# Cross attention with keys on partitions, scores made twice, in one loop with the experts

## The chip, the core and the metric

The kernel is one program on one core of a Trainium2 chip. It computes a two-layer decoder block by block. The metric is the device time of one execution in microseconds. The change touches the last two blocks of the program; all that comes before them is the same code.

## What is computed

Only the end of the reference matters here: layer 1's cross attention and its experts, each followed by a residual and a layer norm (post-norm). There are 8 sequences (B = 8) of 256 tokens (S) with 512 channels (D). x is the decoder's state, ctx the context, both 256 x 512 for a sequence.

The cross attention runs over channels, not over tokens: `_L1_xattn_ref` reads q, k and v as (sequence, 256 rows, 512 columns), splits the 256 rows into 8 heads of 32, and attends from the 512 columns of q to the 512 columns of k:

```
qh = q.reshape(B, h, 32, 512); kh, vh alike (k = v = ctx)
qk = einsum('bhdq,bhdl->bhql', qh, kh) / sqrt(32)
ret = einsum('bhql,bhdl->bhdq', softmax(qk), vh)      # 8 heads, 512 x 512 scores each
x = layernorm(x + gamma * ret)
```

The experts (`_L1_ffn_ref`) project each token with 8 router columns and 8 x 16 hidden columns (136 in all), take a softmax over the 8, keep the best 2, scale the hidden values by the gates, multiply by a 128 x 512 matrix, add biases, and the result goes through residual and layer norm once more.

## The kernel before

Every engine has its own hand-written instruction list, which runs in order; semaphores tie the lists together. The blocks follow one another with a barrier of all engines between two of them.

**Cross attention, `l1_cross` (L1794).** A tile is 128 rows of x, that is 4 heads (HT = 4); a sequence has T = 2 tiles. Exact products are made by splitting fp32 numbers into a rounded part (hi) and the rest (lo); `stack` (L1877) copies them by 32 DMAs per sequence on SyncE's queue into qs and ks, four blocks of 32 rows on top of each other, so that one fp32r matmul with 128 rows gives the exact score. A sequence has STEPS = 16 steps. A step takes 256 queries of one head: `scores` (L2090) makes two 128 x 512 blocks with the queries on partitions; VectorE's `maxima` (L2013) reduces 1024 columns to two negated maxima; ScalarE's `exps` (L1965) makes exp(s - max) with accumulated row sums; two steps later TensorE turns the 8 blocks p by transposes (`turn`, L2100), ScalarE and VectorE copy half each to SBUF (L1973, L2020), and `values` (L2124) multiplies them in fp32, four heads packed on 32-column tiles, in parts spread over the steps. At the end of a tile the reciprocals of 16 sums per partition (L2025) are spread over columns by small matmuls (L2109), `scale_out` multiplies (L2031) and adds the residual (L2036), statistics (L221, L225) and `apply` (L239) normalise, GpSimd takes the power (L231, L233), and SyncE stores x to DRAM. Score PSUM has two buffers of two banks; v_ps and m_ps have one bank each.

**Experts, `l1_experts`.** Its loads begin behind the barrier. Per sequence: `turn_x` (L2373, 8 transposes), copies (L2255), `project` (L2382, 8 fp32 matmuls of 136 columns), `shift` (L2284 to L2289), `exponential` (L2260), `route` (L2295 to L2330), `turn_hidden` (L2390), copies (L2266, L2267), `out` (L2399, L2400: 4 fp32 matmuls of 512 columns), residual (L2341), norm, store.

A fp32 matmul stands in the trace as two records, a transpose or an fp32r matmul as one.

## Time and profile before

| | us |
|---|---|
| median of 3 runs | 2082.64 (2082.24 to 2092.4) |
| the profiled execution | 2083.66 |
| its span, first to last instruction | 2081.9 |
| TensorE, VectorE, ScalarE, GpSimd busy in the span | 1846.4, 1249.2, 920.4, 288.0 |
| cross block, from 1629.75; experts block, first instruction at 1993.88 | to 1990.75; to 2081.9 |

Engines are named PE (TensorE matmuls), PEld (its weight loads), DVE (VectorE), ACT (ScalarE), POOL (GpSimd) and SPq (SyncE's DMA queue). Matmul ends are modelled, so a matmul's real spacing is read from the starts. "Idle before" names what ended the wait. The granted clock is a share of 2.4 GHz; 0.5 is the lower of its two levels, 1.2 GHz.

### The profile page before, as it was taken

Reading aid. Unit: us, or ns where it says so; the run is one execution under the profiler, and the core shown is the slowest. Engines: PE = TensorE matmul, PEld = TensorE weight load, DVE = VectorE, ACT = ScalarE, POOL = GpSimd, SP = SyncE. Lnnn points to the kernel's source line nnn. Section 1 sums busy time; section 2 is a strip of 40 time slices with the busy share of each in tenths; the row PEclk is TensorE's granted clock in tenths of the full one; section 3 lists DMA queues with packets and bytes.
Section 4 is the critical chain, followed back from the end, with each engine's and each line's share of the span. In section 5 each row is a group of like instructions: output and inputs, shape, how many; then the busy total and the mean of one; then the engine's idle time right before and its main releaser. Section 6 shows DMA issues by size and latency. Waiting matters only on the chain. (4 is left out here: it accounts for less than half of the span.)

```text
span 2081.9 us, 33021 instructions
## 1 busy us (share of the span) xinstructions
PE 1846.4 (89%) x12272; PEld 1503.4 (72%) x12272; DVE 1249.2 (60%) x2330; ACT 920.4 (44%) x2376; POOL 288.0 (14%) x347
## 2 busy tenths in 40 slices
PE   6979999999976799999999996799997498889966
PEld 5868999998964588888888985677775365555543
DVE  3446444444434565546555536788887288878847
ACT  2224333333323343333333223666666288878811
POOL 0000000000002111111111001333343111121001
PEclk9989999999997799999999998999998699999988
DMA  3122000000013231111101013000010675556234
GB/s 104 45 97 72 21 21 21 21 21 21 10 48 101 66 97 47 36 31 41 46 19 34 11 41 121 11 31 32 31 42 21 182 179 136 153 140 149 68 114 142
DMA packets 86253, 136.62 MB, mean 66 GB/s; under 512 B 9480, under 2 KB 25480, under 8 KB 86096
## 3 DMA queue, kind: packets, MB, share of 16 engines
q1 hardware_dynamic: 86096, 134.52, 22.3%
q8 instruction: 99, 1.62, 0.3%
q14 instruction: 58, 0.48, 0.1%
HBM read 79.88 MB, written 21.05 MB: 48 GB/s over the span
## 5 line engine op out<-in xcount | busy, mean ns | idle before, releaser
L1164 PE MATMUL yp<-ccy,toep 128*128 128x288 f32 x640 | 182.4, 436 | 19.5 <-POOL ccy L892 13.4
L1965 ACT ACTIVATE e_p<-e_s_ps,e_nb 128x512 f32<-128x512 f32 x256 | 175.0, 696 | 51.6 <-DVE e_nb L2013 49.5
L2013 DVE TENSOR_REDUCE e_nb<-e_s_ps 128x2 f32<-128x1024 f32 x128 | 155.8, 1218 | 54.3 <-PE e_s_ps L2090 53.5
L1442 ACT ACTIVATE p<-p,nb,rq 128x128 f32<-128x128 f32 (+1 forms) x256 | 137.0, 541 | 94.5 <-DVE nb L1539 94.5
L2100 PE MATMUL e_t_ps<-ident,e_p 128*128 128x128 f32 x1024 | 148.7, 284 | 24.7 <-DVE e_pT L2020 13.2
L1164 PEld LDWEIGHTS yp<-ccy,toep 128*128 128x128 f32 x640 | 126.5, 206 | 55.7 <-POOL ccy L892 14.8
L2100 PEld LDWEIGHTS e_t_ps<-ident,e_p 128*128 128x128 f32 x1024 | 120.8, 146 | 62.5 <-issue 52.9
L80 PE MATMUL q_ps<-a_xt_hi,wq_hi 128*128 128x256 f32 x512 | 151.7, 296 | 4.1 <-DVE wo_lo L112 4.1
L1062 DVE SCALAR_TENSOR_TENSOR hm<-gu_ps,us_col,sg 128x256 f32<-128x256 f32 x88 | 42.3, 481 | 182.3 <-ACT sg L971 182.3
L82 PE MATMUL q_ps<-a_xt_hi,wq_lo 128*128 128x256 f32 x512 | 146.5, 286 | 0.0
L81 PE MATMUL q_ps<-a_xt_lo,wq_hi 128*128 128x256 f32 x512 | 146.4, 286 | 0.0
L514 ACT ACTIVATE ex<-ex 128x512 f32<-128x512 f32 x64 | 40.5, 632 | 213.8 <-DVE ex L567 213.8
L231 POOL TENSOR_TENSOR n_rstd<-n_mv,eps 128x2 f32<-128x2 f32 x32 | 6.3, 197 | 895.9 <-DVE n_mv L225 895.9
L971 ACT ACTIVATE sg<-gu_ps,gs_col 128x256 f32<-128x256 f32 x88 | 41.6, 473 | 188.3 <-PE gu_ps L82 188.3
L545 DVE TENSOR_TENSOR tl<-t_ps,th 128x512 fp32r<-128x512 f32 x64 | 44.3, 692 | 132.6 <-ACT th L506 132.6
L1399 POOL TENSOR_TENSOR p<-p,rs 128x512 f32<-128x512 f32 x64 | 94.2, 1472 | 194.5 <-DVE rs L1546 194.5
L2090 PE MATMUL e_s_ps<-ks,qs 128*128 128x512 f32 x256 | 97.5, 464 | 12.6 <-DMA ks<-e_cl 11.5
L80 PE MATMUL o_ps<-wo_hi,th 128*128 128x512 f32 x256 | 106.7, 417 | 1.9 <-DVE tl L545 1.9
L80 PE MATMUL gu_ps<-m_xt_hi,wg_hi 128*128 128x256 f32 x352 | 100.2, 285 | 8.2 <-DVE m_xt_lo L1054 8.2
L567 DVE TENSOR_SCALAR ex<-q_ps,bq_col 128x256 f32<-128x256 f32 x128 | 55.8, 477 | 80.0 <-PE q_ps L82 80.0
L80 PEld LDWEIGHTS q_ps<-a_xt_hi,wq_hi 128*128 128x128 f32 x512 | 99.8, 195 | 4.5 <-issue 4.5
L81 PE MATMUL o_ps<-wo_lo,th 128*128 128x512 f32 x256 | 101.2, 395 | 0.0
(277 smaller groups left out, 5122.1 us busy)
## 6 DMA issues: line engine op xcount, KB each, us to landing
x_after<-n_r SPq DMA_DIRECT2D x24, 512.0 KB, 3.0
toep<-padded_kernels SPq DMA_DIRECT2D x32, 256.0 KB, 3.5
qs<-e_xh SPq DMA_DIRECT2D x64, 128.0 KB, 2.5
qs<-e_xl SPq DMA_DIRECT2D x64, 128.0 KB, 2.6
ks<-e_ch SPq DMA_DIRECT2D x64, 128.0 KB, 2.6
ks<-e_cl SPq DMA_DIRECT2D x64, 128.0 KB, 2.6
x<-x_after SPq DMA_DIRECT2D x12, 512.0 KB, 4.7
x<-in_x SPq DMA_DIRECT2D x8, 512.0 KB, 4.1
```

What stands on the lines that cost most here:

```text
L80: pe.matmul(out, whi, xhi, start=start, stop=False)
L81: pe.matmul(out, whi, xlo, start=False, stop=False)
L82: return pe.matmul(out, wlo, xhi, start=False, stop=stop)
L545: dve.tensor_tensor(tl[:], t_ps[:], th[:], ALU.subtract).then_inc(tl_done, 1)
L567: dve.tensor_scalar(ex[p % 2][:, h, :], q_ps[p % 2][:, h, :], bq_col[:, head:head + 1], 0.0, ALU.add, ALU.min).then_inc(mq_done, 1)
L1164: last = pe.matmul(yp[:, lo % 2, 0:NCOL], toep[h % 2][:, (lo - li) * P:(lo - li + 1) * P], ccy[h % 2][:, li, 0:NCOL], start=(li == 0), sto ...
L1399: pool.tensor_tensor(tile, tile, r, ALU.mult).then_inc(pn_done, 1)
L1442: act.activation(p[n % 3][:, h, part[t]], p[n % 3][:, h, part[t]], ACT.Exp, bias=nb[i][:, t, h:h + 1], scale=rq[u][:, t:t + 1], accum_out= ...
L1965: act.activation(pr[i][:, a, :], s_ps[i][:, a, :], ACT.Exp, bias=nb[i][:, a:a + 1], accum_out=sums[t][:, j, q:q + 1]).then_inc(e_done, 1)
L2013: dve.tensor_reduce(nb[i][:], s_ps[i][:], AX.X, ALU.max, negate=True).then_inc(nb_done, 1)
L2090: last = pe.matmul(s_ps[i][:, a, :], qs[u][:, h // HT, h % HT, q * P:(q + 1) * P], ks[u][:, h // HT, h % HT, :], start=True, stop=True)
L2100: last = pe.transpose(t_ps[a][:, k, :], pr[m % 2][:, a, k * P:(k + 1) * P], core.ident[:])
```

## The change

`l1_cross` and `l1_experts` become one function with one loop, `l1_cross_and_experts`. Scores are made twice. The rough pair: two fp32r matmuls of the rounded parts alone (32 rows, on 32-row tiles) with queries on partitions, only for `maxima`. The negated maxima are turned by 4 transposes per tile (`turn_largest`), rounded by ScalarE, and written by 4 row DMAs on ScalarE's queue (`place_largest`) into row 97 of qs, against a row of ones in ks. The exact scores (97 rows, three blocks: hi hi, lo hi, hi lo, and the maximum) are then made with keys on partitions, so that `exps` makes p already turned and needs neither bias nor accumulation. `values` multiplies it (4 fp32 matmuls) and `ones` (4 more) gives the sums, in d_ps; both banks are single. VectorE's `normalise` takes a reciprocal of 128 x 512 and one product.

A sequence has again 16 steps. At step g TensorE issues the rough pair of step g+11, the two score matmuls of step g, and at odd steps `values` for four earlier score blocks. The rough pairs share two PSUM buffers (a_ps) with all the rest: context, maxima, x, hidden, turned and out. They alternate in the order of `slot_uses`; `take` waits until the last use of the buffer has been read. Of the diff, the core (VectorE's and ScalarE's unchanged helpers are left out):

```diff
-STEPS = HX * NQ // 2
-HALF = STEPS // 2
+STEPS = T * NQ * HT // 2
+UNITS = 2 * STEPS
+LEAD = 11
+NPT = 12
+KX = 3 * CX + 1
...
+        a_ps = [pb(f"e_a_ps{i}", [P, 2, D]) for i in range(2)]
+        s_ps = [pb(f"e_s_ps{i}", [P, D]) for i in range(2)]
+        v_ps, d_ps = pb("e_v_ps", [P, D]), pb("e_d_ps", [P, D])
...
+        def steps():
+            for b in range(-1, B + 2):
+                for step in range(STEPS):
+                    g = STEPS * b + step
+                    if -LEAD <= g <= STEPS * (B + 1) + 5:
+                        yield b, step, g
...
+                def stack(b):
...
+                    for j in range(HT):
+                        for dst, plan in ((qs, (xh[b % 2], xl, xh[b % 2])), (ks, (ch[b % 2], ch[b % 2], cl))):
+                            for r, src in enumerate(plan):
...
             @block.gpsimd
             def _(pool):
...
+                for b, step, g in steps():
+                    if step == 3 and 0 <= b - 2 < B:
+                        power(b - 2, mv6, mv6_done, y6_done, rstd6, ve6_done, rstd6_done)
+                    if step == 3 and 0 <= b - 1 < B:
+                        residual(b - 1, 1)
+                    if step == 6 and 0 <= b - 1 < B:
+                        power(b - 1, mv5, mv5_done, y5_done, rstd5, ve5_done, rstd5_done)
+                    if step == 6 and b + 2 < B:
+                        scale_x(b + 2)
+                    if step == 10 and b + 2 < B:
+                        take_lo(pool, b + 2, "cl")
+                    if step == 11 and 0 <= b < B:
+                        residual(b, 0)
+                    if step == 12 and b + 2 < B:
+                        take_lo(pool, b + 2, "xl")
...
             @block.scalar
             def _(act):
...
+                def place_largest(n):
...
+                    for j in range(HT):
+                        act.dma_start(qs[b % 2][KX - 1:KX, t, j, :].bitcast(F32),
+                                      nbr[n % 2][j * CX:j * CX + 1, :].bitcast(F32)).then_inc(biased, 16)
...
+                for b, step, g in steps():
+                    if step == 1 and 0 <= b - 2 < B:
+                        hidden(b - 2)
+                    if step in (6, 14) and 0 <= 2 * b + 1 + step // 8 < 2 * B:
+                        place_largest(2 * b + 1 + step // 8)
+                    if 0 <= g < PAIRS_IN_ALL:
+                        exps(2 * g)
+                        exps(2 * g + 1)
+                    if step == 4 and 0 < b + 1 < B:
+                        context(b + 1)
+                    if step in (5, 13) and 0 <= 2 * b + 1 + step // 8 < 2 * B:
+                        round_largest(2 * b + 1 + step // 8)
+                    if step == 9 and 0 <= b - 1 < B:
+                        turned(b - 1)
+                    if step == 9 and b + 2 < B:
+                        round_hi(b + 2, "ch")
+                    if step == 11 and b + 2 < B:
+                        round_hi(b + 2, "xh")
+                    if step == 12 and 0 <= b - 1 < B:
+                        exponential(b - 1)
...
             @block.vector
             def _(dve):
...
+                def normalise(n):
+                    dve.wait_ge(pv_mm, NQ * (n + 1))
...
+                    dve.reciprocal(rec[:], d_ps[:]).then_inc(rec_done, 1)
...
+                    dve.scalar_tensor_tensor(rb[n % 2][:], v_ps[:], gcol[:, 0:1], rec[:], ALU.mult, ALU.mult)\
+                       .then_inc(o_scaled, 1)
...
+                for u in range(2):
+                    dve.memset(ks[u][KX - 1:KX, :, :, :].bitcast(F32), 1.0).then_inc(set_up, 1)
+                take_lo(dve, 0, "cl")
+                take_lo(dve, 0, "xl")
...
+                for b, step, g in steps():
+                    if step == 2 and 0 <= b - 2 < B:
+                        add_experts(b - 2)
+                    if step == 11 and 0 <= b - 1 < B:
+                        shift(b - 1)
+                    if 0 <= g + LEAD < PAIRS_IN_ALL:
+                        maxima(g + LEAD)
+                    if b == 0 and step == 0:
+                        dve.wait_ge(w_loaded, 64)
...
+                    if step in (2, 10) and 0 <= 2 * b - 1 + step // 8 < 2 * B:
+                        normalise(2 * b - 1 + step // 8)
+                    if step == 2 and 0 <= b - 2 < B:
+                        statistics(b - 2, added6, b - 1, st6, st6_done, mv6, mv6_done)
+                    if step == 4 and 0 <= b - 2 < B:
+                        apply(b - 2, mv6, rstd6, rstd6_done, y6_done)
+                    if step == 5 and 0 <= b - 1 < B:
+                        statistics(b - 1, added5, T * b, st5, st5_done, mv5, mv5_done)
+                    if step == 7 and 0 <= b - 1 < B:
+                        apply(b - 1, mv5, rstd5, rstd5_done, y5_done)
+                    if step == 13 and 0 <= b - 1 < B:
+                        gate(b - 1)
+                        choose(b - 1)
+                    if step == 14 and 0 <= b - 1 < B:
+                        picks(b - 1)
+                        weigh(b - 1)
...
             @block.tensor
             def _(pe):
...
+                def take(kind, n, *freed):
+                    i = place[kind, n] % 2
+                    if read[i]:
+                        pe.wait_ge(*read[i])
+                    read[i] = freed
+                    return a_ps[i]
...
+                def rough_scores(n):
...
+                    bank = take("pair", n, nb_done, n + 1)
+                    for i in range(2):
+                        j = 2 * jj + i
+                        d = slice(j * CX, (j + 1) * CX)
+                        last = pe.matmul(bank[:, i, :], xh[b % 2][d, t, q * P:(q + 1) * P], ch[b % 2][d, t, :],
+                                         start=True, stop=True, skip_group_check=True, tile_position=(j * CX, 0))
...
+                def scores(u):
...
+                    if u >= 2:
+                        pe.wait_ge(e_done, u - 1)
+                    pe.matmul(s_ps[u % 2][:], ks[b % 2][0:KX, t, j, k * P:(k + 1) * P], qs[b % 2][0:KX, t, j, :],
+                              start=True, stop=True).then_inc(s_mm, 1)
...
+                def values(n):
+                    b, t, k, _ = unit(HT * n)
+                    pe.wait_ge(e_done, HT * (n + 1))
+                    if k == 0 and n:
+                        pe.wait_ge(o_scaled, T * b + t)
...
+                for b, step, g in steps():
+                    if 0 <= g + LEAD < PAIRS_IN_ALL:
+                        rough_scores(g + LEAD)
+                    if 0 <= g < PAIRS_IN_ALL:
+                        scores(2 * g)
+                        scores(2 * g + 1)
+                    if g == 1:
+                        pe.wait_ge(set_up, 5)
+                    if g % 2 and 0 <= (g - 3) // 2 < T * NQ * B:
+                        values((g - 3) // 2)
+                    if step == 1 and 0 <= b - 2 < B:
+                        out(b - 2)
+                    if step == 3 and 0 < b + 1 < B:
+                        turn_context(b + 1)
+                    if step in (5, 13) and 0 <= 2 * b + 1 + step // 8 < 2 * B:
+                        turn_largest(2 * b + 1 + step // 8)
+                    if step == 8 and 0 <= b - 1 < B:
+                        turn_x(b - 1)
+                    if step == 10 and 0 <= b - 1 < B:
+                        project(b - 1)
+                    if step == 15 and 0 <= b - 1 < B:
+                        turn_hidden(b - 1)
```

The store of x behind the cross attention and its reload are gone: the residual stays in SBUF (rr). The router's weights and biases are loaded behind the first sequence's stack.

## Rows read from the trace of the kernel before

**Rows 1.** Windows: length, busy PE, PEld, DVE, ACT, POOL, clock, DMA share, GB/s
```profile
1629.00:1986.00 357.00, 301.60 (x2368) 191.56 (x2368) 273.23 (x346) 277.19 (x688) 57.48 (x38) 0.93 0.55 139
1986.00:2082.00 96.00, 62.30 (x288) 41.26 (x288) 58.51 (x241) 15.46 (x40) 8.85 (x21) 0.84 0.41 138
```

**Rows 2.** Groups by line, cross block: count, busy us, mean ns, idle before
```profile
L1965 ACT ACTIVATE e_p<-e_s_ps,e_nb 128x512 f32<-128x512 f32 x256 | 175.0, 696 | 51.6 <-DVE e_nb L2013 49.5 <-PE e_t_ps L2100 1.8
L2013 DVE TENSOR_REDUCE e_nb<-e_s_ps 128x2 f32<-128x1024 f32 x128 | 155.8, 1218 | 54.3 <-PE e_s_ps L2090 53.5 <-ACT e_p L1965 0.6
...
L2020 DVE COPY e_pT<-e_t_ps 128x512 f32<-128x512 f32 x128 | 87.2, 681 | 10.6 <-PE e_t_ps L2100 10.6
L1973 ACT ACTIVATE e_pT<-e_t_ps 128x512 f32<-128x512 f32 x128 | 77.5, 605 | 13.1 <-PE e_t_ps L2100 12.4
...
L1965 ACT ACTIVATION_READ_ACCUMULATOR e_p<-e_s_ps,e_nb 128x1 f32 x256 | 54.3, 212 | 0.0
```

**Rows 3.** Timeline, two steps of cross attention: start us, duration us, instruction
```profile
1955.15 0.30 PEld L2090 LDWEIGHTS e_s_ps<-ks,qs 128*128 128x128 f32 x2 [0.84 <-ACT e_p L1965]
...
1955.92 1.22 DVE L2013 TENSOR_REDUCE e_nb<-e_s_ps 128x2 f32<-128x1024 f32 x1 [0.74 <-PE e_s_ps L2090]
...
1958.45 0.16 PEld L2124 LDWEIGHTS e_v_ps<-e_pT,e_vt 128*32 128x32 f32 x8 [0.17 <-issue]
...
1958.52 0.59 ACT L1973 ACTIVATE e_pT<-e_t_ps 128x512 f32<-128x512 f32 x1
...
1959.00 0.70 ACT L1965 ACTIVATE e_p<-e_s_ps,e_nb 128x512 f32<-128x512 f32 x1
1959.44 0.30 PEld L2090 LDWEIGHTS e_s_ps<-ks,qs 128*128 128x128 f32 x2 [0.84 <-ACT e_p L1965]
```

**Rows 4.** TensorE behind two idle times (timeline), and a window behind the first
```profile
1781.95 1.93 PE L2124 MATMUL e_v_ps<-e_pT,e_vt 128*32 128x512 f32 x8 [3.17 <-DVE n_r L2036]
...
1782.00:1790.00 8.00, 8.00 (x37) 4.70 (x38) 5.30 (x6) 5.21 (x14) 0.00 (x0) 0.62 0.82 189
...
1930.48 0.63 PE L2100 MATMUL e_t_ps<-ident,e_p 128*128 128x128 f32 x4 [1.29 <-DVE e_pT L2020]
1931.04 1.07 PE L2124 MATMUL e_v_ps<-e_pT,e_vt 128*32 128x512 f32 x8
```

**Rows 5.** Timeline, experts: routing's first and last, copy, project, statistics
```profile
2012.23 0.17 DVE L2295 TENSOR_REDUCE f_den<-f_ex 128x2 f32<-128x16 f32 x1 [0.58 <-ACT f_ex L2260]
...
2015.09 0.49 DVE L2330 SCALAR_TENSOR_TENSOR f_hw<-f_lh,f_w 128x128 f32<-128x128 f32 x2
...
2024.50 1.08 ACT L2255 ACTIVATE f_xT<-f_x_ps 128x512 f32<-128x512 f32 x2 [4.34 <-PE f_x_ps L2373]
...
2025.64 2.12 PE L2382 MATMUL f_h_ps<-wrd,f_xT 128*128 128x136 f32 x16 [0.30 <-ACT f_xT L2255]
...
2025.87 1.27 DVE L221 BATCH_NORM_STATS2 n_stats<-n_r 128x6 f32<-128x512 f32 x2
```

**Rows 6.** Timeline, the last tile's values, back to back
```profile
1981.95 3.62 PE L2124 MATMUL e_v_ps<-e_pT,e_vt 128*32 128x512 f32 x32
```

**Rows 7.** Timeline, scores of four heads on 32-row tiles in the block before
```profile
1501.69 0.94 PE L1701 MATMUL s_ps<-kT,qT 32*128 32x128 f32 x16
```

**Rows 8.** An issue on SyncE's queue (timeline), and a DMA: KB, us to landing
```profile
1642.31 0.60 SPq L1886 DMA_DIRECT2D qs<-e_xh  x1
...
f_bias<-in_bd SPq DMA_DIRECT2D x1, 64.0 KB, 6.0
```

**Rows 9.** Groups by line: the reciprocals of 4 and of 16 columns
```profile
L1546 DVE RECIPROCAL rs<-sums 128x4 f32<-128x4 f32 x64 | 10.7, 168 | 0.2 <-ACT p L1442 0.2
L2025 DVE RECIPROCAL e_rs<-e_sums 128x16 f32<-128x16 f32 x16 | 3.9, 243 | 0.0
```

**Rows 10.** Timeline, the cross block's start: the last lo part, the first scores
```profile
1634.56 2.46 POOL L1866 TENSOR_TENSOR e_xl<-x,e_xh 128x1024 fp32r<-128x1024 f32 x1 [2.72 <-ACT e_xh L1948]
...
1644.22 0.93 PEld L2090 LDWEIGHTS e_s_ps<-ks,qs 128*128 128x128 f32 x3 [8.43 <-DMA ks<-e_cl]
```

More of the change, by code:

```diff
@@ new lines, in slot_uses @@
+        def slot_uses(b, step, g):
+            if 0 <= g + LEAD < PAIRS_IN_ALL:
+                yield "pair", g + LEAD
+            if step == 1 and 0 <= b - 2 < B:
+                yield "out", b - 2
+            if step == 3 and 0 < b + 1 < B:
+                yield "context", b + 1
+            if step in (5, 13) and 0 <= 2 * b + 1 + step // 8 < 2 * B:
+                yield "largest", 2 * b + 1 + step // 8
+            if step == 8 and 0 <= b - 1 < B:
+                yield "x", b - 1
+            if step == 10 and 0 <= b - 1 < B:
+                yield "hidden", b - 1
+            if step == 15 and 0 <= b - 1 < B:
+                yield "turned", b - 1
@@ new lines, in l1_cross_and_experts, with slot, unit, pair @@
+        place = {("context", 0): 0}
+        for at in steps():
+            for use in slot_uses(*at):
+                place[use] = len(place)
+        def slot(kind, n):
+            return a_ps[place[kind, n] % 2]
+        def unit(u):
+            b, rest = divmod(u, UNITS)
+            t, rest = divmod(rest, UNITS // 2)
+            return b, t, rest // HT, rest % HT
+        def pair(n):
+            b, rest = divmod(n, STEPS)
+            t, rest = divmod(rest, STEPS // 2)
+            return b, t, rest // 2, rest % 2
@@ L2269, in body @@
-                def body(b, u, first, last):
-                    if not last:
-                        turned(b + 1, 1 - u)
-                    if not first:
-                        hidden(b - 1, 1 - u)
-                    exponential(b)
-                turned(0, 0)
-                over_batches(act, body, lambda b, u: hidden(b - 1, 1 - u))
+                    if b:
+                        act.wait_ge(o_mm, b)
+                    bank = slot("turned", b)
+                    act.activation(hwT[:], bank[:, 0, 0:S], ACT.Copy).then_inc(hT_done, 1)
@@ L2344, in body @@
-                def body(b, u, first, second):
-                    shift(b, u)
-                    if not first and not second:
-                        norm.apply(dve, b - 2)
-                    route(b)
-                    if not first:
-                        residual(b - 1, 1 - u)
-                dve.wait_ge(w_loaded, 64)
-                dve.tensor_scalar(bias[:, 0, 0:E], bias[:, 0, 0:E], BONUS, None, ALU.add).then_inc(prepared, 1)
-                dve.wait_ge(prepared, 3)
-                def tail(b, u):
-                    norm.apply(dve, b - 2)
-                    residual(b - 1, 1 - u)
-                    norm.apply(dve, b - 1)
@@ L2360, in _, with add_experts @@
-                for b in range(B):
-                    body(b, b % 2, b == 0, b == 1)
-                tail(B, 0)
+                def add_experts(b):
+                    dve.wait_ge(o_mm, b + 1)
+                    dve.tensor_tensor(rr[b % 2][:], slot("out", b)[:], rr[b % 2][:], ALU.add).then_inc(added6, 1)
+                for u in range(2):
+                    dve.memset(ks[u][KX - 1:KX, :, :, :].bitcast(F32), 1.0).then_inc(set_up, 1)
+                take_lo(dve, 0, "cl")
+                take_lo(dve, 0, "xl")
@@ new lines, in turn_x, with project @@
+                def turn_x(b):
+                    pe.wait_ge(y5_done, T * b + T)
+                    bank = take("x", b, xT_done, b + 1)
+                    for k in range(KT):
+                        for t in range(T):
+                            last = pe.transpose(bank[:, k // 2, (k % 2 * T + t) * P:(k % 2 * T + t + 1) * P],
+                                                rr[b % 2][:, t, k * P:(k + 1) * P], core.ident[:])
+                    last.then_inc(x_turned, 1)
+                def project(b):
+                    pe.wait_ge(xT_done, b + 1)
+                    pe.wait_ge(w_loaded, 64)
+                    bank = take("hidden", b, lh_done, b + 1)
+                    n = E + E * R
```

656 lines of the change are left out of this document (250 added, 406 removed).

## The prediction

> **What bounds the kernel now.** I read the windows first: the cross attention block takes 357 us and the experts 96 us of a span of 2081.9 us [rows 1]; what comes before 1629 us is untouched. Then the groups by line in the cross block: ScalarE carries most, 175.0 us of exponentials, 54.3 of accumulator reads (partly beside them) and 77.5 of copies; VectorE has 155.8 us of maxima and 87.2 of copies [rows 2]. Then two steps of the loop in order of time [rows 3]: they take 4.29 us (weights of the scores at 1955.15 and 1959.44), and the circle is score pair, maximum of 1.22 us, exponentials, copy. TensorE does its transposes and values beside it. From the first scores at 1644.2 [rows 10] to the last values at 1985.6 [rows 6] eight sequences take 42.7 us each; the experts add 12 each with their start and end.
>
> **The change part by part.** It removes per step 8 transposes, both p copies and the accumulator reads; per sequence 8 of 32 stack DMAs and x's store and reload; and one block's start and end. It adds per step a rough pair (R), per two steps 8 fp32 matmuls for values and sums (V, 4 before), per sequence two reciprocals of 128x512, 8 transposes and 8 row DMAs for the maxima, and puts the experts into the same loop. So the time has to be made anew: I walk one sequence of 16 steps, each engine in its written order. P(s) is the start of TensorE's step s.
>
> *Prices, TensorE.* Four packed value matmuls cost 0.86 us (32 records of 16 matmuls in 3.62 us, less the last one's drain) [rows 6], 0.99 up to the next full tile's weights [rows 3]; so V is 1.71 and 0.14 for the change of tile. Two score matmuls are 0.47 and 0.1 of exposed weights. R is not in the trace. Its bounds are 0.47, two serial 512-column matmuls, and 0.235, two at once. The nearest row has four heads on 32-row tiles: 16 records, 3072 columns at two cycles, in 0.94 us where one after the other would take 2.56 at 2.4 GHz [rows 7]. They overlap, so I take 0.235, and 0.27 for two changes of tile. A step without V (E) is then 1.06 us of TensorE, one with V (O) 2.9. Eight transposes are 1.0, project 2.0 [rows 5], out 8 records of 0.43, 3.45.
>
> *ScalarE.* An exponential without accumulation lasts 0.6 and the next starts 0.48 later, as the copies [rows 3]; a product is read 0.29 us after its stream (pair weights 1955.15, read 1955.92). With two score banks the last two scores of an E,O pair wait for exponentials: +0.44, so a pair takes 4.4 us. A 1024-column copy is 1.08 [rows 5], the two hidden ones 0.7. The row DMAs of the maxima are issued ahead of exponentials; SyncE's issues take 0.60 for 32 rows [rows 8], below could be nought; I take 0.4 each for a single row, 1.6 for four.
>
> *VectorE.* A maximum (m) is 1.22, so 1.04 ns a column (1218 against 681 ns) [rows 2]; adding 1024 columns 1.25; statistics 1.66; apply 1.0; shift 0.9; gates to weights 3.4 [rows 5]. *Reciprocal:* 4 columns take 168 ns, 16 take 243 [rows 9], 6.25 ns a column more, so 512 take 0.243+496x0.00625=3.35 us. Its bounds are an ordinary pass of 0.68 and 243/16 ns a column, 7.8 us. I take 3.35, the only slope shown. With the product N=3.35+0.06+0.69=4.1.
>
> *The full sequence.* R leads TensorE's queue and shares two slots, so a late reader stops everything: the lead of 11 steps in data is none in slots.
> Steps 10, 11: m ends at 1.8, N at 5.9. TensorE does E, project, R and scores by 4.2; then V opens a new tile and waits for o_scaled, since v_ps and d_ps are single. P(12)=P(10)+7.85.
> 12 to 15: two pairs 8.8, maxima's transposes 0.55, hidden's 0.55, ScalarE's DMA issues 1.55: 11.45. VectorE, with routing in steps 13 and 14, keeps up.
> 0: R of step 1 needs the slot of "turned", which ScalarE copies behind two exponentials: 2.7.
> 1: O and out, 6.45.
> 2, 3: add to 1.45, m to 2.65, N to 6.75, statistics to 8.4, m to 9.6, for which R of step 4 waits; V waits for N (6.8+1.75+context 1.0): 9.65.
> 4: R of step 5 waits for the context copy behind two exponentials, 3.1. Step 5: 3.45. Steps 6, 7: 4.4+1.55. Steps 8, 9 with turn x and the wait for its copy: 5.2.
> The sum is 55.8 us. GpSimd's pieces, under 3 us each like the one in [rows 10], end before their readers' steps; if a residual were late, only statistics would move. SyncE's 24x0.64=15.4 us of stack issues are hidden in a sequence.
>
> *Ends.* The block starts at 1629.75. VectorE first fills two rows of 4096 columns, 4.2 us each at 1.04 ns (one partition; nought if faster), then makes both lo parts, ready at 1640.7 instead of 1637.0 [rows 10]. The stacks are issued by 1656.2; 8 maxima, transposes, copy, issues and landing end about there too: P(0)=1657. Sequence 0 takes 49.5, of it 6.5 for VectorE's wait at step 0 for the router's bias, issued last, with 6.0 to land [rows 8]. Sequence 1 takes 50.1 (no out, no hidden copies), 2 to 6 take 279, 7 takes 48.3 (no R behind step 4). Then the serial chain N, statistics, apply, turn, project, route, out, statistics, store: 43. Sum 2126.9, with 1.8 around the span 2128.7.
>
> *Clock.* Behind 3.17 us of idle the values take 1.93 us instead of 1.07 and the granted clock is 0.62 over the next 8 us; behind 1.29 us nothing falls [rows 4]. The walk has TensorE idle for 4.7 us in step 3 of sequences 1 to 7, and 1.8 in step 11. V and context at 1.2 GHz cost 2.7 more and the rest of the step 0.3: 7x3.0=21. For step 11, between the two rows, I put 0.7x8: together 27. Forecast: 2155 us, against 2083.66 of the profiled run (median 2082.64).
>
> **The rivals.** (1) *Cheap normaliser and free DMA issues.* With an ordinary-speed reciprocal N is 1.45: 16x2.65=42 off; with free issues 15x1.55=23 off; no clock drops: 2064, faster. For it: every reciprocal in the trace is tiny. Against: 243 ns for 16 columns is above such a floor, and an issue has always had a price on SyncE. It decides once N is under about 2.3 us, where V no longer waits in step 11. (2) *The cheap normaliser alone:* 2087, no change. (3) *No clock falls,* other waits breaking up the idle: 2129. Against: 3.17 us was enough. (4) *R doesn't overlap:* its matmuls run one after the other, 0.235 more in 128 steps, some hidden in ScalarE's waits, 26: 2181. [rows 7] speaks against. (5) *The rough pair truly runs ahead and nothing waits,* so that TensorE's own work sets the time, 8x41 us a sequence between 1657 and 43 of tail: 2030. The single v_ps speaks against, and the maxima behind N. (6) *The reciprocal's slope is hidden by a floor:* 4-column ones may stand at it, and eight ordinary passes, 8.3 ns a column, are 4.4 us: 16 more, 2171.
> The Trainium skill, VectorE: DVE Perf Modes, in "First, the fixed hardware budget", says that reciprocal is an iterative divide with a repeat count of 8. That would be rival 6; no row here shows a wide reciprocal.
>
> **How the numbers follow.** Forecast 0.50; rival 6 0.15; rival 3 0.13; rival 4 0.08; rival 2 0.05; rivals 1 and 5 together 0.09. Upwards the reciprocal's upper bound adds 16x4.5=72 (2227), DMA issues of 0.6 add 12. The range of 2080 to 2225 leaves out rivals 1 and 5 and what lies above. A measurement of this kernel tells 0.5%, 10 us, from no change. Faster, under 2072: 0.10; within: 0.06; slower: 0.84.
>
> **What would show it.** In the profile after: two reciprocals a sequence of 3.35 us each; V's weights idle until the normaliser is done, 4 to 5 us in step 3 and about 2 in step 11; R held by maxima and by ScalarE's copies; about 56 us from one sequence to the next; first scores at 1657; a granted clock below 1 behind step 3. It fails if a sequence takes under 50 us (cheap reciprocals, or the waits overlap better than a walk in single file has them), if R takes 0.5 us, or if ScalarE's exponentials don't feel the DMA issues.

## The result and the profile after

The changed kernel takes 2219.16 us (median, 2213.76 to 2229.92), the kernel before 2086.91 us beside it: a ratio of 1.064, 95% interval 1.059 to 1.069. It is slower by 132 us, on the side that the prediction gave 0.84, and inside its range, 6 us below the upper end. The forecast of 2155 is 64 us too low. The profiled execution is the slowest of them, 2229.92 us with a span of 2228.1.

The groups by line of the new block (count, busy us, mean ns, idle before and its releaser) show first what carries it. The reciprocals answer to [rows 9], the maxima and exponentials to [rows 2]:

```profile
L2147 DVE RECIPROCAL e_rec<-e_d_ps 128x512 f32<-128x512 f32 x16 | 53.6, 3349 | 11.2 <-PE e_d_ps L2332 11.2
...
L2141 DVE TENSOR_REDUCE e_nbx<-e_a_ps 128x2 f32<-128x1024 f32 x128 | 154.2, 1222 | 188.9 <-PE e_a_ps L2299 188.7
L2085 ACT ACTIVATE e_pT<-e_s_ps 128x512 f32<-128x512 f32 x256 | 139.1, 595 | 318.7 <-PE e_s_ps L2317 277.7
```

VectorE and ScalarE both wait for TensorE now. The windows of the first sequence's start and of four full sequences (length, then busy PE, PEld, DVE, ACT and POOL, clock, DMA share, GB/s) answer to [rows 1]:

```profile
1657.00:1701.00 44.00, 31.68 (x122) 11.18 (x122) 13.39 (x13) 14.69 (x26) 8.88 (x4) 0.67 0.67 175
1832.00:1903.00 71.00, 56.78 (x248) 21.90 (x248) 36.84 (x56) 23.13 (x42) 12.53 (x10) 0.78 0.30 75
1903.00:1971.00 68.00, 53.78 (x245) 20.62 (x244) 36.62 (x54) 22.79 (x42) 10.85 (x10) 0.80 0.31 78
1971.00:2039.00 68.00, 53.61 (x243) 20.32 (x242) 36.28 (x55) 22.54 (x41) 10.35 (x10) 0.80 0.26 63
2039.00:2107.00 68.00, 53.80 (x246) 20.66 (x245) 36.52 (x55) 21.87 (x41) 7.29 (x8) 0.80 0.26 63
```

A sequence takes 68.2 us where the walk had 55.8, at a mean granted clock of 0.80 against 0.93 before. The clock has two levels, so 0.80 means that TensorE stood at 1.2 GHz for 40% of the time, some 27 of 68 us. TensorE's part of the timeline (start us, duration us, instruction, the idle time before it with its releaser) shows where, from step 10 of one sequence to step 8 of the next:

```profile
1907.14 1.55 PE L2329 MATMUL e_v_ps<-e_pT,e_vt 128*32 128x512 f32 x8 [1.85 <-DVE e_rb L2151]
1908.39 2.01 PE L2332 MATMUL e_d_ps<-e_pT,e_ones 128*32 128x512 f32 x8
...
1913.16 1.07 PE L2329 MATMUL e_v_ps<-e_pT,e_vt 128*32 128x512 f32 x8
1914.05 1.04 PE L2332 MATMUL e_d_ps<-e_pT,e_ones 128*32 128x512 f32 x8
...
1919.52 0.98 PE L2317 MATMUL e_s_ps<-qs,ks 97*128 97x512 f32 x2 [2.33 <-ACT e_pT L2085]
...
1921.37 1.96 PE L2332 MATMUL e_d_ps<-e_pT,e_ones 128*32 128x512 f32 x8
...
1927.10 0.50 PE L2299 MATMUL e_a_ps<-e_ch,e_xh 32*128 32x512 f32 x2 [1.49 <-ACT f_wT L2106]
...
1928.23 1.94 PE L2329 MATMUL e_v_ps<-e_pT,e_vt 128*32 128x512 f32 x8
...
1941.92 1.93 PE L2329 MATMUL e_v_ps<-e_pT,e_vt 128*32 128x512 f32 x8 [4.02 <-issue]
...
1949.47 0.50 PE L2299 MATMUL e_a_ps<-e_ch,e_xh 32*128 32x512 f32 x2 [1.95 <-ACT e_vt L2061]
...
1950.57 1.06 PE L2329 MATMUL e_v_ps<-e_pT,e_vt 128*32 128x512 f32 x8
...
1956.94 0.98 PE L2317 MATMUL e_s_ps<-qs,ks 97*128 97x512 f32 x2 [2.33 <-ACT e_pT L2085]
...
1966.01 1.94 PE L2329 MATMUL e_v_ps<-e_pT,e_vt 128*32 128x512 f32 x8
```

These are the waits of the walk, in their places: the values of steps 11 and 3 for the normaliser (1.85 and 4.02 us), the rough pairs of steps 1 and 5 for ScalarE's copies (1.49 and 1.95), the scores of steps 15 and 7 for exponentials that stand behind four DMA issues (2.33 each). The rows at full clock (1913.16) have values and sums from start to start in 1.86 us. Behind the waits they take up to 3.44. Windows behind the last three waits, in the same columns as above:

```profile
1941.00:1945.00 4.00, 3.08 (x16) 0.68 (x16) 3.45 (x7) 0.00 (x0) 1.55 (x3) 0.50 0.01 2
1945.00:1958.00 13.00, 8.72 (x52) 3.88 (x52) 8.07 (x12) 5.29 (x10) 3.35 (x4) 0.99 0.48 163
1958.00:1969.00 11.00, 11.00 (x48) 4.18 (x42) 2.45 (x2) 4.59 (x8) 0.29 (x1) 0.54 0.00 0
```

So not only the wait of 4 us brings the clock down: behind the 2.33 us of step 7 it is at 0.54 for 11 us, in which TensorE never rests. Nor does every wait bring it down: the 1.95 us of step 5 end at 1949.47, inside the window with 0.99, and the values behind take 1.06 us. That is so in four of the sequences 2 to 6; in the other (the wait that ends at 1879.74) the clock is 0.57 from 1880 to 1884. Of the 12.4 us that a sequence takes above the walk, the start-to-start times give 10.1 to slow products (1.3 in step 11, 1.2 in step 15, 1.6 in step 1, 1.6 in step 3, 0.8 in step 7, 3.6 in steps 8 and 9). ScalarE's issues are the second part; the walk had 1.55 for each four:

```profile
1916.34 2.43 ACTq L2078 DMA_DIRECT2D qs<-e_nbr  x4
```

The four issues take 2.43 us, 0.9 more than the walk had, twice a sequence: 1.8. Here, with the 4.02 us for which the profile names no releaser ("issue"; they are the wait for the normaliser, since the reciprocal of 1937.68 and the product behind it end just before the values start), the reading of one trace ends, and the experiments begin.

### The profile page after: what moved, and what is told of

Read it like the earlier page. It is cut to its first block and busy times, and to the rows that moved or that the text cites. A ratio compares the mean times of both kernels' runs of the same rounds, so it can differ in the third digit from the quotient of the medians.

```text
span 2228.1 us, 30727 instructions
## 1 busy us (share of the span) xinstructions
PE 1925.5 (86%) x11568; PEld 1442.3 (65%) x11568; DVE 1221.4 (55%) x2181; ACT 812.0 (36%) x1976; POOL 306.0 (14%) x365
## 5 line engine op out<-in xcount | busy, mean ns | idle before, releaser
L2141 DVE TENSOR_REDUCE e_nbx<-e_a_ps 128x2 f32<-128x1024 f32 x128 | 154.2, 1222 | 188.9 <-PE e_a_ps L2299 188.7
L2085 ACT ACTIVATE e_pT<-e_s_ps 128x512 f32<-128x512 f32 x256 | 139.1, 595 | 318.7 <-PE e_s_ps L2317 277.7
L2317 PE MATMUL e_s_ps<-qs,ks 97*128 97x512 f32 x256 | 112.9, 511 | 40.7 <-ACT e_pT L2085 37.7
L2329 PE MATMUL e_v_ps<-e_pT,e_vt 128*32 128x512 f32 x512 | 96.3, 833 | 42.9 <-issue 27.2
L2299 PE MATMUL e_a_ps<-e_ch,e_xh 32*128 32x512 f32 x256 | 76.0, 590 | 41.4 <-DVE e_nbx L2141 16.1
L2317 PEld LDWEIGHTS e_s_ps<-qs,ks 97*128 97x128 f32 x256 | 45.9, 212 | 91.6 <-ACT e_pT L2085 56.5
L2299 PEld LDWEIGHTS e_a_ps<-e_ch,e_xh 32*128 32x128 f32 x256 | 28.1, 215 | 115.3 <-issue 66.5
```

What stands on the lines that cost most here:

```text
L2085: act.activation(pT[u % NPT][:], s_ps[u % 2][:], ACT.Exp).then_inc(e_done, 1)
L2141: dve.tensor_reduce(heads, slot("pair", n)[:], AX.X, ALU.max, negate=True).then_inc(nb_done, 1)
L2299: last = pe.matmul(bank[:, i, :], xh[b % 2][d, t, q * P:(q + 1) * P], ch[b % 2][d, t, :], start=True, stop=True, skip_group_check=True, ti ...
L2317: pe.matmul(s_ps[u % 2][:], ks[b % 2][0:KX, t, j, k * P:(k + 1) * P], qs[b % 2][0:KX, t, j, :], start=True, stop=True).then_inc(s_mm, 1)
L2329: pe.matmul(v_ps[j * CX:(j + 1) * CX, :], vt[b % 2][:, k, e:e + CX], pT[(HT * n + j) % NPT][:], start=(k == 0), stop=(k == NQ - 1), skip_g ...
```

## The experiments

Theory A: the waits are as walked; what was missed is that TensorE falls to 1.2 GHz behind each of five or six waits of 1.5 to 4 us, not behind one. Rivals: the clock is low for other reasons or costs nothing (B), or the order of TensorE's queue, with the rough pair in front, is the cause. "Less" and "more" are against the median of the changed kernel, 2219.16 us, where nothing else is said.

### More work in the waits

`idle_work` issues fp32 matmuls of 512 columns into the free half bank of the next slot:

```diff
+                    if step in (7, 15) and 1 <= b < B - 1:
+                        idle_work("pair", g + LEAD + 1, 2) if step == 7 else idle_work("turned", b - 1, 2)
...
+                    if step == 3 and 1 <= b < B - 1:
+                        idle_work("context", b + 1, 4)
+                    if step == 11 and 1 <= b < B - 1:
+                        idle_work("pair", g + LEAD + 1, 2)
```

> The changed kernel (2219 us) with more work on TensorE that nothing reads: fp32 matmuls of 512 columns (about 0.86 us each at the full clock) into a free half bank, four ahead of the values of step 3, two each ahead of the values of steps 7, 11 and 15, in six sequences: 60 matmuls, 52 us of TensorE's time at full clock. Nothing is left out. Theory A (the clock falls behind TensorE's idle waits of 1.5 to 4 us): the waits are filled, the granted clock in the middle sequences rises from 0.80 to 0.9 or more, and the time is lower although the work is more: 6x5 to 6x10 us off, about 2160 to 2190. Rival B (the clock isn't what costs; or it falls whatever TensorE does in a wait): the clock stays at 0.80 and the time rises, by up to 52 us (2271) where the work doesn't fit into the waits.

Measured: 2202.34 us (1.055 of before, 1.049 to 1.060), 17 less than the changed kernel, with 60 matmuls more. Two sequences of this run in windows, and the fills of step 3 and step 11 in its timeline:

```profile
1858.00:1925.00 67.00, 60.23 (x266) 23.61 (x264) 36.63 (x54) 22.94 (x41) 10.85 (x9) 0.87 0.35 87
1925.00:1988.00 63.00, 56.10 (x266) 22.04 (x264) 36.76 (x54) 22.95 (x41) 10.88 (x9) 0.95 0.33 82
```

```profile
1927.99 3.70 PE L2380 MATMUL e_a_ps<-f_wu,ident 128*128 128x512 f32 x8
1932.08 1.07 PE L2329 MATMUL e_v_ps<-e_pT,e_vt 128*32 128x512 f32 x8 [0.39 <-issue]
...
1961.14 1.98 PE L2380 MATMUL e_a_ps<-f_wu,ident 128*128 128x512 f32 x4 [2.11 <-DVE f_lh L2174]
```

The wait for the normaliser is filled with 3.70 us of work, and the values behind it take 1.07 us, not 1.93. The clock of the sequences is 0.87 to 0.95, not 0.80, and one takes 62.5 to 67 us. That the time falls when work is added speaks for A and is nothing that the recorded rival B allows. Of its size, 17 and not 30 to 60, the trace shows a part: in step 11 the fill itself waits 2.11 us, for VectorE to read its slot, and only then does its 1.98 us of work ahead of the values, so it comes on top of a wait instead of filling it. The waits of steps 1 and 5 were not filled. What this run can't tell apart is a wait and a lightly used TensorE as such, since a fill changes both.

### One wait at a time

The row DMAs of the maxima on SyncE's queue:

```diff
-                    if step in (6, 14) and 0 <= 2 * b + 1 + step // 8 < 2 * B:
-                        place_largest(2 * b + 1 + step // 8)
+                    if step == 14 and b == -1:
+                        place_largest(0)
...
+                    place_largest(2 * b + 1)
+                    if b + 1 < B:
+                        place_largest(2 * b + 2)
```

> The changed kernel (2219 us) with the row DMAs of the maxima issued from SyncE's queue instead of ScalarE's, but for the first four. Nothing is left out. Theory A (ScalarE's four issues, 2.43 us in the trace, hold its exponentials, and the values wait for those): 14 to 15 times 2.4 us off, 34, and the idle of 2.3 us in steps 7 and 15 gone, so a higher clock, 1 to 3 us a sequence more: about 2170. Rival B (something else releases the values at the same time, or the rows now come late behind SyncE's stack issues, and the scores wait for them): no change or slower, 2215 to 2240.

Measured: 2151.87 us (1.031 of before, 1.028 to 1.035), 67 less. By the expectation the issues themselves were 34 of them; the other 33 are put down to the clock, which rose, and they are more than A expected. A sequence of this run, with the columns as before (two earlier ones have 0.88):

```profile
2006.00:2065.00 59.00, 49.39 (x256) 19.33 (x258) 37.92 (x55) 22.14 (x41) 4.35 (x6) 0.91 0.25 60
```

ScalarE's three copies ahead of the step's two exponentials:

```diff
-                    if step == 1 and 0 <= b - 2 < B:
-                        hidden(b - 2)
+                    if step == 0 and 0 <= b - 2 < B:
+                        hidden(b - 2)
+                    if step == 4 and 0 < b + 1 < B:
+                        context(b + 1)
+                    if step == 9 and 0 <= b - 1 < B:
+                        turned(b - 1)
```

(the lines of context and turned behind the exponentials go).

> The changed kernel (2219 us) with one edit: ScalarE's copies of the hidden layer, of the context and of x transposed stand ahead of the two exponentials of the step, not behind them. Nothing is left out. Theory A (two of TensorE's idle stretches a sequence, 1.5 us in step 1 and 1.95 us in step 5, are waits for these copies, and one of 1.95 us was enough to bring the granted clock to 0.5 for the next 6 us): 8x3.4=27 less by the waits and 2 to 4 us a sequence more by the clock, about 2170, with the clock of the middle sequences above 0.80. Rival B (the wait is only moved, as the exponentials that the values wait for are later by 0.7 and 1.1 us; the clock doesn't follow waits as short as these): 2205 to 2219 at a clock of 0.80.

Measured: 2182.30 us (1.045, 1.043 to 1.047), 37 less, at a clock of 0.85 to 0.86 between 1800 and 2100 us where the changed kernel has 0.81. It lies between the theories, nearer to A: 27 are the waits by A's own account, which leaves 10 for the clock instead of 16 or more. Part of these come in step 7, whose wait of 2.3 us is still there: in the sequence of 1926.37 to 1938 the clock behind it is 0.53 up to 1931 and 1.00 from there on, where the changed kernel stays low for about 10 us.

VectorE's normaliser ahead of the addition, the shift and the maximum:

```diff
+                    if step in (2, 10) and 0 <= 2 * b - 1 + step // 8 < 2 * B:
+                        normalise(2 * b - 1 + step // 8)
                     if step == 2 and 0 <= b - 2 < B:
                         add_experts(b - 2)
```

> The changed kernel (2219 us) with VectorE's normaliser at the head of steps 2 and 10, ahead of the experts' addition, the shift and the maximum of that step. Nothing is left out. Theory A: the values of steps 3 and 11 find their tile free 2.6 and 1.8 us sooner, but the maxima are as much later, and the rough pair that waits for them leads TensorE's queue. In step 11 up to 1.8 us a sequence is won (the rough pair then has a slot to spare), in step 3 nothing in the period (the maximum of step 3 ends where it did), but the idle is broken in two and the clock falls less: 2219-8x1.8-7x1=about 2198. Rival B (the rough pair's slots decide in both): the wait moves from the values to the rough pair, and the time stays at 2219 or is up to 10 us more.

Measured: 2191.65 us (1.052, 1.048 to 1.055), 28 less, near A's number, but not in A's places. In step 3, where A saw nothing to win in the period, the wait is now 0.69 us and the rough pair's, and the values run at full clock. In step 11, where A had its 1.8 us, the rough pair now waits 2.38 us for a late maximum, as rival B has it, and the values behind it are slow:

```profile
1860.10 0.49 PE L2299 MATMUL e_a_ps<-e_ch,e_xh 32*128 32x512 f32 x2 [0.69 <-DVE e_r L2232]
1860.53 0.73 PE L2317 MATMUL e_s_ps<-qs,ks 97*128 97x512 f32 x2
1861.19 1.06 PE L2329 MATMUL e_v_ps<-e_pT,e_vt 128*32 128x512 f32 x8
...
1890.94 0.50 PE L2299 MATMUL e_a_ps<-e_ch,e_xh 32*128 32x512 f32 x2 [2.38 <-DVE e_nbx L2141]
...
1892.38 1.94 PE L2329 MATMUL e_v_ps<-e_pT,e_vt 128*32 128x512 f32 x8
```

The reciprocal on 16 columns alone (this kernel leaves the division out for the other 496):

```diff
-                    dve.reciprocal(rec[:], d_ps[:]).then_inc(rec_done, 1)
+                    dve.reciprocal(rec[:, 0:16], d_ps[:, 0:16]).then_inc(rec_done, 1)
```

> The changed kernel (2219 us) with the reciprocal of the sums made for 16 of the 512 columns alone; the rest of the factors is 1.0, so the division is left out for them. The normaliser falls from 3.35+0.06+0.75=4.16 us to about 0.25+0.06+0.75=1.06. Theory A (the waits are as walked, and the rest of the miss is TensorE's clock behind each of them): steps 2 and 3 lose about 3.1 us a sequence, steps 10 and 11 about 1.7, 8x4.8=38, and the tail 3; besides, two of the five idle stretches a sequence go, so the granted clock in the middle sequences rises from 0.80 to 0.85 or more and gives 2 to 4 us a sequence more: 2219-41-24=about 2150, and the period under 64 us. Rival B (the clock is low for another reason, say the lighter use of TensorE by itself): the clock stays at 0.80 and the time at about 2178. Rival C (VectorE's reciprocal was hidden behind ScalarE): no change, 2219.

Measured: 2177.66 us (1.044, 1.039 to 1.049), 41.5 less. In total that is what the waits were walked to be worth (41), and rival B's number: the clock gave nothing. In the full sequences it even took some back: they fell by 3.4 us, from 68.2 to 64.8, not by 4.8, at a clock of 0.76. Two sequences and a later stretch in windows, and what stands behind one of the waits that are left in the timeline:

```profile
1847.00:1912.00 65.00, 55.83 (x246) 21.82 (x246) 30.28 (x55) 22.94 (x41) 10.95 (x9) 0.76 0.33 82
1912.00:1977.00 65.00, 55.83 (x247) 21.81 (x245) 30.26 (x55) 22.94 (x41) 10.96 (x9) 0.76 0.32 82
...
2025.00:2040.00 15.00, 13.28 (x62) 5.02 (x62) 5.15 (x6) 5.39 (x12) 0.00 (x0) 1.00 0.79 173
```

```profile
1866.77 1.28 PE L2320 MATMUL e_s_ps<-qs,ks 97*128 97x512 f32 x2 [2.23 <-ACT e_pT L2086]
...
1877.01 1.94 PE L2332 MATMUL e_v_ps<-e_pT,e_vt 128*32 128x512 f32 x8
```

The wait of 0.91 us in step 3 of this run is followed by values at full clock in four sequences, but behind the 2.23 us of step 7 every product is slow for over 12 us. The 1.95 us of step 5, mostly harmless in the changed kernel, are followed by low stretches here, and two waits late in the run, 2.33 us up to 2024.96 and 1.50 us up to 2030.98, by none (the window of 2025 to 2040 has 1.00), while behind 0.92 us up to 2041.07 the values take 1.94. So A has to be put more narrowly. Most waits of 1.5 us and more are followed by a stretch at 1.2 GHz, but not all, and how long it lasts differs from wait to wait (about 3 us to 13 us); with two of six waits gone, others had longer stays. What decides both wasn't settled: the length of the wait alone does not, and the price of one wait can't be read off another.

### The place of the rough pair in TensorE's queue

Behind the scores (first run), or behind scores and values (second run), where the change has it in front:

```diff
-                    if 0 <= g + LEAD < PAIRS_IN_ALL:
-                        rough_scores(g + LEAD)
                     if 0 <= g < PAIRS_IN_ALL:
                         scores(2 * g)
                         scores(2 * g + 1)
+                    if 0 <= g + LEAD < PAIRS_IN_ALL:
+                        rough_scores(g + LEAD)
```

> The changed kernel (2219 us) with each step's rough pair issued behind the step's two score products and ahead of its values. Nothing is left out. Theory A (the rough pair's waits for a slot, 1.5 to 2.0 us in steps 1, 4 and 5, hold the scores and so the exponentials that the values need): the scores of these steps start during that wait, the exponentials run beside it, and 1 to 2 us each come off: 8x3=24, and a higher clock: about 2190. Rival B (the values stand behind the rough pair as before, and TensorE waits as long, only between other products): no change, 2210 to 2225. Rival C (the maxima start 0.7 us later in every step, and the rough pair two steps on waits for them): up to 8x3=24 slower, 2243.

Measured: 2218.82 us (1.063, 1.059 to 1.068), rival B: no change. The rough pair's wait in step 5 fell from 1.95 to 0.52 us, but the values now wait 2.52 us for the normaliser in step 11 instead of 1.85, and the scores of steps 7 and 15 2.95 instead of 2.33.

> The changed kernel (2219 us) with each step's rough pair issued behind the scores and behind the values. Nothing is left out. Theory A (the place of the rough pair in TensorE's queue costs, as every wait of it holds the products behind): the scores and values never wait for a slot of a rough pair of their own step; about 2180, below the run with the rough pair in the middle. Rival B (the same few waits, in particular the values for the normaliser, now hold the rough pair and so VectorE's maxima, whose next rough pair then comes late): 2219 or slower, up to 8x6=48, since in step 3 the maximum no longer runs beside the values.

Measured: 2207.65 us (1.059, 1.055 to 1.063), 11.5 less. The interval overlaps the changed kernel's (1.059 to 1.069), so this is at most a part of A. The order isn't what makes the change slow.

### Taking the waits away together

The kernel with the rows on SyncE's queue, and with the values' two tiles read out at once. The same run also has the router's bias treated at step 7 of the first sequence, the rows of ones filled by GpSimd and the statistics moved to other steps; the diff shows the first two parts:

```diff
-                    dve.reciprocal(rec[:], d_ps[:]).then_inc(rec_done, 1)
...
+                    dve.tensor_scalar(rb[n % 2][:], v_ps[:], gcol[:, 0:1], None, ALU.mult).then_inc(v_read, 1)
...
+                    act.activation(rec[:], d_ps[:], ACT.Copy).then_inc(d_read, 1)
...
+                    part = slice(i * (D // 2), (i + 1) * (D // 2))
+                    dve.reciprocal(rec[:, part], rec[:, part]).then_inc(rec_done, 1)
...
+                        pe.wait_ge(v_read, T * b + t)
+                        pe.wait_ge(d_read, T * b + t)
```

> The changed kernel (2219 us; 2152 with the row DMAs of the maxima on SyncE's queue) with four things together; nothing is left out. The row DMAs are on SyncE's queue. The tiles of the values and of the sums are read out at once, by one pass of VectorE (0.75 us) and one of ScalarE (0.6 us), and the reciprocal is taken later from the copy, in two halves, one each in steps 3 and 4 (11 and 12), with the statistics and their ends moved two steps back. The router's bias is treated at step 7 of the first sequence instead of step 0. The two rows of ones are filled by GpSimd. Theory A (the waits of the walk are what costs, and the clock follows them): the wait for the normaliser of about 4 us in step 3 and 1.9 in step 11 falls to under 1 us, 8x5=40, with 2 to 4 us a sequence by the clock, 6.5 at the first step and 7 at the head: 2152-40-20-13=about 2080, no slower than the kernel before (2087). Rival B (the reciprocals' halves make maxima late instead, and the rough pair leads the queue): half of it is lost, 2110 to 2130.

Measured: 2102.22 us (1.007, 1.003 to 1.010), 50 less than with the rows alone. About 11 of the 50 are the earlier start (first scores at 1652.07 against 1662.92); the parts have no runs of their own. The wait for the normaliser is gone in steps 3 and 11, and the clock of the middle stretches is 0.91 to 0.95. A expected 2080 and B 2110 to 2130; it lies between.

On top of this the three copies ahead of the exponentials, with the edit shown above:

> The kernel of e7_release with three of ScalarE's copies (hidden, context, x transposed) put ahead of the two exponentials of the step behind which they stood. Nothing is left out. Theory A (the rough pairs of steps 1, 5 and 10 wait for a slot that ScalarE copies only behind two exponentials, 1.5 to 2 us each): 8x3=24 less than e7_release, and more by the clock. Rival B (the exponentials are what the values wait for, and they are now later by the copy, 0.7 to 1.1 us): 0 to 8x2=16 more than e7_release.

Measured: 2086.67 us (1.000, 0.999 to 1.002), 15.5 less, nearer to A. With this, the change costs nothing against the kernel before.

The lead of 12 (`LEAD = 12`, with the transposes of the maxima in steps 4 and 12), and the last tile's chain ahead of the experts' addition:

```diff
+                    if step == 2 and b == B:
+                        invert(2 * B - 1, 0)
+                        invert(2 * B - 1, 1)
+                        scale_values(2 * B - 1)
```

> The kernel of e8_copies (2087 us) with the rough pair a step further ahead (12 instead of 11), so that the maxima are transposed in steps 4 and 12 and their row DMAs issued a step sooner; the row DMAs of the second half of the first sequence are on ScalarE's queue, and behind the last tile VectorE takes the reciprocal and the statistics of the cross attention ahead of the experts' addition and statistics of the sequence before. Nothing is left out. Theory A (in e8_copies TensorE waits 9.5 us in step 8 of the first sequence and 2.4 us in step 8 of the others for these rows, half of a sequence's clock falls come from there, and the last chain stands 5 us behind other work): 8 + 7x2.4 + 5 less and 1 us a sequence by the clock, against 1.2 at the head: about 2052, faster than the kernel before (2087) by 1.6%. Rival B (the scores of step 8 are late for another reason): 2087-8-5=2074.

Measured: 2069.39 us (0.991, 0.989 to 0.993), 17 less than e8_copies, where A had 35 and B 13. The first sequence's long wait and the end gave what they should, the full sequences nothing: a step more of lead made the transposes earlier, but not the DMAs. ScalarE's copy of the rows, SyncE's queue, and TensorE's scores of step 8:

```profile
1808.31 0.62 ACT L2093 ACTIVATE e_nbr<-e_a_ps 128x512 fp32r<-128x512 f32 x1
...
1811.87 0.36 SPq L1956 DMA_DIRECT2D e_xr<-x_after  x1
...
1813.36 2.47 SPq L1975 DMA_DIRECT2D qs<-e_nbr  x4
...
1819.02 0.70 PE L2363 MATMUL e_s_ps<-qs,ks 97*128 97x512 f32 x2 [3.01 <-issue]
```

The rows are ready at 1808.9, but SyncE's queue stands at the load of x for the residual (e_xr) until GpSimd's residual is done, as the last experiment's expectation sets out. The same kernel with the rough pair last, edit as above:

> The kernel of e9_lead12 with each step's rough pair issued behind the scores and the values. Nothing is left out. Theory A (in the changed kernel this order won 11 us, 2208 against 2219, as scores and values no longer stand behind a rough pair that waits): up to 8x1.5=12 less than e9_lead12. Rival B (once nothing waits for slots, the order only makes the maxima later by 0.7 to 2.6 us, and transposes and scores follow them): the same time or up to 15 us more than e9_lead12.

Measured: 2102.13 us (1.006, 1.004 to 1.008), 33 more than e9_lead12. Where the order was worth at most 11.5 us to the other side in the changed kernel, it costs 33 once the other waits are gone: more than rival B had. Two waits of TensorE a sequence carry most of it: the scores of step 8 wait 4.8 to 5.1 us for their rows in sequences 1 to 4, where e9_lead12 has 3.0 to 3.7, and the hidden layer's transposes wait 2.4 us for VectorE's routing, where e9_lead12 has no such wait:

```profile
1832.31 1.19 PE L2363 MATMUL e_s_ps<-qs,ks 97*128 97x512 f32 x2 [4.77 <-issue]
...
1857.12 0.33 PE L2408 MATMUL e_a_ps<-ident,f_hw 128*128 128x128 f32 x1 [2.40 <-DVE f_hw L2260]
```

And last, the row DMAs ahead of x's reload on SyncE's queue:

```diff
+                    if b:
+                        place_largest(2 * b + 1)
                     if b + 1 < B:
                         residual(b + 1)
```

> The kernel of e9_lead12 (2069 us) with one edit on SyncE's queue: the row DMAs of the second half's maxima stand ahead of the reload of x and the next loads, not behind them. Nothing is left out. In e9_lead12 the rows are copied at 1808.9 us, but SyncE's queue stands at the reload of x, which waits for GpSimd's residual, until 1811.9, and issues the rows at 1813.4 to 1815.8; the scores of step 8 wait 3.0 us for them, and TensorE then runs at the lower clock for about 6 us. Theory A (that wait and the clock behind it are what is left to take): the wait goes, 7x3=21, and 6 us at half the clock are worth 3, 7x3=21 more: about 2030, 2.8% faster than the kernel before, with a clock of 0.98 or more in the middle sequences. Rival B (another wait, such as the slot or the exponentials, stands close behind): half of it, 2050 at a clock of 0.95.

Measured: 2063.07 us against 2083.72 beside it, 0.990 with an interval of 0.988 to 0.991: 1.0% faster than the kernel before. Against e9_lead12 (0.991) that is no difference that the intervals show. Neither number was reached. The wait for the rows is gone, and right behind it stands another, of the same step:

```profile
1815.98 1.10 PE L2390 MATMUL e_a_ps<-ident,e_r 128*128 128x128 f32 x8 [2.71 <-DVE e_r L2202]
1817.12 0.50 PE L2344 MATMUL e_a_ps<-e_ch,e_xh 32*128 32x512 f32 x2
1817.55 1.13 PE L2364 MATMUL e_s_ps<-qs,ks 97*128 97x512 f32 x2
1818.61 1.94 PE L2377 MATMUL e_v_ps<-e_pT,e_vt 128*32 128x512 f32 x8
```

x's transposes wait for the normalised x, whose statistics e7_release put back by a step. That is rival B's mechanism; the values behind the 2.71 us are slow (1.94 us), as products behind the 3.01 us were.

## Why the prediction was right, and where it was off

*The reciprocal and the normaliser.* 3.35 us from the slope of two narrow ones; 3349 ns measured, 6.5 ns a column. Rivals 1 and 2 fall, and so does rival 6 with its 4.4 us. The Trainium skill (VectorE: DVE Perf Modes, "First, the fixed hardware budget") gives the reciprocal a repeat count of 8; read as eight passes, an estimate, that would be rival 6, and the trace doesn't agree. The waits for it came out at 4.02 and 1.85 us against 4.7 and 1.8.

*The rough pair.* The walk had 0.235 for two matmuls at once and 0.27 for the changes of tile, 0.505 together; one after the other they would have made 0.74. They take 0.50 us on the timeline with the next product 0.43 behind the start, so rival 4 falls. The sign "if R takes 0.5 us" was badly put, since the walk's own R was as long.

*The slots and ScalarE's order.* The steps without a fall of the clock came as walked: step 0 2.8 us (2.7), step 4 3.1 (3.1), step 5 3.54 (3.45). First scores at 1658.36 (1657). The wait for the router's bias is there, with 6.14 us on TensorE (6.5).

*The DMA issues of ScalarE.* 0.4 each was taken between nought and 0.6; it is 0.61. The prediction had the price of that, 12 us; with 2.43 us for each four it is 15x0.88=13.

*The clock* is the step that failed. The walk had it as 3.0 us in step 3 and 0.7 in step 11, on the ground that 3.17 us of idle brought a fall and 1.29 none [rows 4]. Between these two rows lie all the other waits that the same walk had found, 1.6 to 2.0 us by its own sums in steps 1, 5, 7 and 15 (1.5 to 2.3 in the trace), and they were given nothing. The trace shows about 10 us a sequence, against 3.7. Over a third of it, 3.6 us, stands in steps 8 and 9, behind the wait of step 7. Over the span the accounts close: the walk without a clock term gives 2126.9, the trace 2228.1, 101 more. Of it 33 are in the first two sequences (the experts' first addition starts at 1799.15; the walk has it at 1657+49.5+50.1+9.2=1765.8), with a clock of 0.72 there, 62 in the next five (341.0 against 279), 6 in the end. Take off 13 for the issues and 1 for the head, and 87 are left for the clock and what the walk didn't have, where the forecast had 27. So the profiled execution, 75 us above the forecast, splits into 60 for the clock and what the walk didn't have, 13 for the issues and 1 for the head. The median is 11 us lower and 64 us above the forecast; it has no such account of its own. That a filled wait makes the products behind it fast and the kernel faster is shown by e2_fill; that the clock is all of the 87 is argued from the start-to-start times, not shown by a run of its own.

*The range.* That 2219 lies inside it is in part luck. Its upper half was there for a dearer reciprocal, a rough pair without overlap and dearer issues. Only the issues came out dearer, by 13 us; what filled the range was the clock behind the other waits, to which no rival gave a price. The sign "about 56 us from one sequence to the next" missed, with 68.2.

Rival 3 (no clock falls, 2129) is refuted. Rival 5, the pair that truly runs ahead, is refuted for the change itself, but the last kernels are on its way: with most waits taken off, a sequence takes 48.7 to 50.1 us (e12_rows_first) against its 41, and the order "rough pair first" is then worth 33 us.

## What to carry to other kernels

When a walk finds waits of an engine whose clock can fall, price each one twice: for its length, and for the slow products that may stand behind it, until a run shows that this wait is harmless in this place. A lead in data is no lead while tiles, slots or a queue in order tie the two ends together. What turned 6% slower into 1% faster here was, in steps that were measured one on top of the other: small DMAs moved off the queue of a busy engine, a tile read out by two cheap copies, copies put ahead of exponentials, and the first sequence's and the last tile's waits. The rough pair's place in front was worth nothing in the changed kernel (last in the queue was, if anything, 11.5 us better), and 33 us once those waits were gone. When one wait goes, look for the next one in the same step before counting the gain: two of the last runs won little, since one stood right behind.

## What the runs showed of the hardware

Most waits of TensorE of 1.5 to 2.3 us were followed by a granted clock of 0.5, as 3.17 had been, but not all: 1.95 us in step 5 of the changed kernel was followed by a clock of 1.00 in four of the five sequences 2 to 6, and in e1_narrow 2.33 us up to 2024.96 by 1.00 as well, while 0.91 us in step 3 of that run was harmless four times and followed by slow values (1.94 us) once. The stay at 1.2 GHz, with TensorE busy all the time, lasted from about 3 us (behind the 4.02 in step 3) to over 12 us (behind 2.23 in e1_narrow), so a short wait can cost more than a long one. A reciprocal of fp32 costs 3349 ns for 512 columns and 1737 for 256 (e9_lead12), at 128 partitions. A DMA issue on ScalarE's queue costs it 0.61 us even for a single row, as on SyncE's, and holds the activations behind it. A fill of one partition with 4096 columns takes 3.47 us on VectorE.
